# Building the one-hots of four groups in seven: slot by slot on GpSimd and turned in two-byte words, instead of compared with broadcast places on VectorE

## What is computed

```python
h = jnp.maximum(_layernorm(x, axis=-1), 0.0)
x = x + jax.ops.segment_sum(h[src], dst, num_segments=6250)
h = jnp.maximum(_layernorm(x, axis=-1), 0.0)
y = out = h
for l in range(3):
    f1 = jax.nn.relu(y[row] @ nb_W[l] + nb_b[l])
    f2 = jax.nn.relu(y[col] @ self_W[l] + self_b[l])
    a = jax.nn.relu(jnp.concatenate([f1, f2], axis=1) @ att1_W[l] + att1_b[l])
    mask = jnp.clip(jax.nn.sigmoid((a @ att2_W[l] + att2_b[l])[:, 0]) * 1.5 - 0.45, 0.0, 1.0)
    rowsum = jax.ops.segment_sum(mask, row, num_segments=n) + 1e-06
    d = jnp.clip(rowsum ** (-0.5), 0.0, 10.0)
    y = jax.ops.segment_sum((mask * d[row] * d[col])[:, None] * y[col], row, num_segments=n)
    out = out + y
x = x + out            # row = src, col = dst
```

## Time and profile before

| | us |
|---|---|
| median of 3 runs (lowest, highest) | 4028.7 (4028.5, 4032.4) |
| the profiled execution | 4025.1 |
| its span in the profile | 4023.2 |
| sort, about | 60 to 480 |
| build and first hop, about | 500 to 1105 |
| three layers, about | 1140 to 4009 |

### The profile page before, as it was taken

How to read it: one execution, slowest core, us unless ns; L and a number is a source line. 1 busy time by engine, 2 the same in 40 slices (tenths; PEclk the granted TensorE clock), 3 DMA queues, 4 the chain that set the end, 5 groups by cost and what they waited for, 6 DMA issues and landing times. The chain is left out here.

```text
span 4023.2 us, 257999 instructions
## 1 busy us (share of the span) xinstructions
PE 3711.7 (92%) x99855; PEld 3565.5 (89%) x99856; DVE 3262.2 (81%) x5362; ACT 1976.7 (49%) x5432; POOL 2380.6 (59%) x4693
## 2 busy tenths in 40 slices
PE   5999678888879999999998999999998999999998
PEld 4888578888859999899988999999997999989998
DVE  7999868888768888788877888878886888878887
ACT  1222368888721111488871111178884111138887
POOL 2777523333235666677774666667775566667776
PEclk8989799999989999999999999999999999999999
DMA  1111189999837777677745777757773677767775
GB/s 38 16 16 16 26 282 335 342 339 338 308 100 249 248 240 244 196 190 190 191 133 193 244 248 248 249 158 190 190 191 120 234 247 240 245 198 190 191 190 153
DMA packets 586269, 800.05 MB, mean 199 GB/s; under 512 B 126790, under 2 KB 528154, under 8 KB 586170
## 3 DMA queue, kind: packets, MB, share of 16 engines
q1 hardware_dynamic: 550106, 719.89, 57.3%
q0 software_dynamic: 36064, 78.85, 6.6%
HBM read 672.34 MB, written 126.04 MB: 198 GB/s over the span
## 5 line engine op out<-in xcount | busy, mean ns | idle before, releaser
L1372 PE MATMUL pre_ps<-rows_a,hot_ab 128*128 128x64 bf16 x21609 | 1298.3, 193 | 46.7 <-ACT rows_a L1465 23.2
L1372 PE MATMUL pre_ps<-table,hot_ab 128*128 128x64 bf16 x21609 | 1296.9, 193 | 1.1 <-issue 1.1
L1372 PEld LDWEIGHTS pre_ps<-rows_a,hot_ab 128*128 128x128 fp8e4 x21609 | 1128.2, 98 | 75.9 <-issue 52.8
L1606 POOL TENSOR_TENSOR message<-message 128x448 f32<-128x448 f32 x1029 | 947.2, 932 | 318.3 <-DVE message L1674 317.7
L1372 PEld LDWEIGHTS pre_ps<-table,hot_ab 128*128 128x128 fp8e4 x21609 | 1130.8, 98 | 0.6 <-issue 0.6
L1656 DVE SCALAR_TENSOR_TENSOR message<-pre_ps,all_w 128x448 f32<-128x448 f32 x1029 | 642.8, 625 | 276.9 <-PE pre_ps L1372 200.3
L1416 PE MATMUL pre_ps<-table,hot_ab 128*128 128x64 bf16 x21609 | 803.0, 193 | 19.6 <-DVE message L1674 9.0
L1416 PEld LDWEIGHTS pre_ps<-table,hot_ab 128*128 128x128 fp8e4 x21609 | 761.7, 98 | 22.1 <-issue 21.6
L1513 ACT ACTIVATE message<-pre_ps 128x448 bf16<-128x448 f32 x1029 | 673.6, 675 | 164.9 <-DVE pre_ps L1668 136.7
L1668 DVE TENSOR_TENSOR pre_ps<-pre_ps,mask 128x448 f32<-128x448 f32 x735 | 464.9, 633 | 205.1 <-PE pre_ps L1416 182.9
L1639 DVE TENSOR_REDUCE logit<-message 128x7 f32<-128x448 f32 x1029 | 626.4, 609 | 0.0
(11 more groups left out here) (195 smaller groups left out, 4844.7 us busy)
## 6 DMA issues: line engine op xcount, KB each, us to landing
hot_ab<-hot_scratch SPq DMA_DIRECT2D x2058, 224.0 KB, 4.0
hot_scratch<-hot SPq DMA_DIRECT2D x343, 336.0 KB, 5.9
both<-hot_scratch SPq DMA_DIRECT2D x147, 784.0 KB, 5.1
places<-slots_scratch POOLq DMA_DIRECT2D x196, 224.0 KB, 6.4
places<-slots_scratch POOLq DMA_DIRECT2D x98, 336.0 KB, 7.2
slots_scratch<-bins SPq DMA_DIRECT2D x392, 16.0 KB, 1.4
out<-res SPq DMA_DIRECT2D x1, 1536.0 KB
raw<-in_src SPq DMA_DIRECT2D x1, 768.0 KB
```

The source lines that it names most:

```text
L1372: last = nc.tensor.matmul(pre_ps[g][:, j, :], hot[:, b, g, end, j * P:(j + 1) * P].bitcast(FP8), table, start=end + part == 0, stop=end == ...
L1606: pool.tensor_tensor(message[:, g, :, 2, :], message[:, g, :, 1, :], top[:, g, :, 1, :, 1], ALU.subtract).then_inc(s["third_ready"], 1)
```

## The change

In the groups `COMPARED` = 1, 3, 5 and 6 the row end takes another way.

- *Sort.* ScalarE copies the row half of `bins_ps` a second time, to `row_bins` (bf16); TensorE turns it with an identity (`turn_slots`); ScalarE puts the result into `slot_place`, which keeps for all rows and columns the place of each slot, with the slot on the partition.
- *Build, GpSimd.* `fetch_places` takes one row of `slot_place` (49 values). For each compared unit seven `tensor_scalar` compare `iota1` (1 to 128) with the place of the partition's slot, is-equal and then times 56. That gives part 2, slot by node, directly (`row_slots`). `load` takes the row end of the first group of each chunk alone, and stands behind the compares.
- *TensorE.* In a compared unit `turn` turns part 2 with `pack_two` (128 x 64) into numbers of two bytes, 7 matmuls. `turn_other`, a step later, turns the other end as before, 7 matmuls.
- *VectorE.* `find` compares only the other end (896 bytes). `take_pairs`, a step later, converts the 448 two-byte words to part 0 (`row_nodes`).
- *ScalarE* converts 224 words of such a unit (part 3), and all its jobs, the counts, the sums and the adds come one step later than before.
- SyncE's store waits for `row_slots` and `row_nodes` too.

```diff
                     act.wait_ge(stored[b], nth * (16 * COPIES))
+                    nc.scalar.activation(row_bins[:, b, :], bins_ps[b][0:HALF, :], ACT.Copy)
                     nc.scalar.activation(bins[:, b, :], bins_ps[b][:, :], ACT.Copy).then_inc(s["bins_ready"], 1)
...
+                def turn_slots(c, b):
+                    pe.wait_ge(s["bins_ready"], c + 3)
+                    pe.wait_ge(s["slots_taken"], c + 2)
+                    hold_waits(pe, s)
+                    nc.tensor.matmul(slots_ps[b][:, :], row_bins[:, b, :], k.identb[0:HALF, 0:HALF],
+                                     start=True, stop=True).then_inc(s["slots_turned"], 1)
...
+    COMPARED = (1, 3, 5, 6)
...
                 def load(c, h, r):
                     a, z = chunks[c]
-                    for e in range(2):
-                        tile = k.slots_dram[:, bass.ds(r + e * k.HALF, 1), a * G:z * G, :]
+                    for e, last in ((0, a + 1), (1, z)):
+                        tile = k.slots_dram[:, bass.ds(r + e * k.HALF, 1), a * G:last * G, :]
...
+                def find_slots(n):
+                    if n.g == COMPARED[0]:
+                        fetch_places(n)
+                        pool.wait_ge(s["places_ready"], n.r + 1)
+                    reused(pool, n)
+                    at_least(pool, s["counted"], n.u - NG + 1)
+                    hold_waits(pool, s)
+                    for j in range(G):
+                        last = pool.tensor_scalar(hot[:, n.slot, ROW_SLOT, j * P:(j + 1) * P], k.iota1[:, :], place_of(n, j),
+                                                  float(HOT), ALU.is_equal, ALU.mult)
+                    last.then_inc(s["row_slots"], 1)
...
+                def step(recent):
+                    if recent[0] is not None and recent[0].g in COMPARED:
+                        find_slots(recent[0])
+                    if recent[2] is not None:
+                        next_load(recent[2])
+                each_unit(pool, k, 3, step)
...
                 def turn(n):
                     pe.wait_ge(s["hotT"], n.u + 1)
                     at_least(pe, s["hot_ready"], n.u - 1)
+                    if n.g in COMPARED:
+                        pe.wait_ge(s["row_slots"], compared(n))
...
+                    if n.g in COMPARED:
                         for j in range(G):
+                            last = nc.tensor.matmul(pair_ps[n.half][:, j, :], hot[:, n.slot, ROW_SLOT, j * P:(j + 1) * P].bitcast(FP8),
+                                                    k.pack_two[:, :], start=True, stop=True)
...
+                def turn_other(n):
+                    if n.g in COMPARED:
+                        pe.wait_ge(s["row_nodes"], compared(n))
...
-                    for n, do in zip(recent, (turn, count, add_up)):
+                    for n, do in zip(recent, (turn, turn_other, count, add_up)):
...
-                    for n, do in zip(recent, (take_words, take_counts)):
+                    for n, do in ((recent[1], take_words), (recent[2], take_counts)):
...
+                def take_pairs(n):
+                    if n.g in COMPARED:
+                        dve.wait_ge(s["turned"], n.u + 1)
+                        reused(dve, n)
+                        dve.tensor_copy(hot[:, n.slot, ROW_NODE, :].bitcast(U16), pair_ps[n.half].rearrange("p j w -> p (j w)"))\
+                            .then_inc(s["row_nodes"], 1)
...
-                    for n, do in ((recent[0], find), (recent[3], add_in)):
+                    for n, do in ((recent[0], find), (recent[1], take_pairs), (recent[4], add_in)):
```

More of the change, by code:

```diff
@@ L10 @@
 U8 = mybir.dt.uint8
+U16 = mybir.dt.uint16
 ALU = mybir.AluOpType
@@ L373, in sort_edges @@
         bins_ps = [ps(f"bins_ps{i}", [2 * HALF, P]) for i in range(2)]
+        slots_ps = [ps(f"slots_ps{i}", [P, HALF]) for i in range(2)]
         by_column = hot[:, :, :, :, :].rearrange("p b a g n -> p b (a g) n")
@@ L553, in _ @@
                     dve.sem_inc(s[name], 2)
+                nc.vector.memset(row_bins[:, :, :], 0.0)
                 def pick_blocks(c, b):
@@ L879, in build_and_sum, with compared @@
     WORDS = P // 4
+    ROW_NODE, OTHER_NODE, ROW_SLOT, OTHER_SLOT = range(4)
+    COMPARED = (1, 3, 5, 6)
+    LOADS = [(NB + 1) // 2, (NB + 1) // 2 + 1]
+    def compared(n):
+        before = sum(g < n.g for g in COMPARED)
+        if n.alone:
+            return before + (n.g in COMPARED)
+        return n.i * (2 * len(COMPARED)) + (len(COMPARED) + 2 * before + (n.h + 1) * (n.g in COMPARED))
     chunks = [(a, min(a + 2, NG)) for a in range(0, NG - 1, 2)]
@@ L917, in _ @@
                     load(c, 0, 1)
[L918 to L925, removed]
+                def step(recent):
[4 more added lines that the diff above has]
+                each_unit(pool, k, 3, step)
+                for c in range(len(chunks)):
+                    for h in range(2):
+                        pool.wait_ge(places_in[c][h], LOADS[h] * 32)
             @block.sync
@@ L950, in turn @@
                     at_least(pe, s["hot_ready"], n.u - 1)
+                    if n.g in COMPARED:
+                        pe.wait_ge(s["row_slots"], compared(n))
                     hold_waits(pe, s)
-                    for end in range(2):
+                    if n.g in COMPARED:
                         for j in range(G):
-                            last = nc.tensor.matmul(word_ps[n.half][:, end, j, :],
-                                                    hot[:, n.slot, end, j * P:(j + 1) * P].bitcast(FP8), k.pack[:, :],
-                                                    start=True, stop=True)
-                    last.then_inc(s["turned"], 1)
+                            last = nc.tensor.matmul(pair_ps[n.half][:, j, :], hot[:, n.slot, ROW_SLOT, j * P:(j + 1) * P].bitcast(FP8),
+                                                    k.pack_two[:, :], start=True, stop=True)
+                    else:
+                        for end, of in enumerate((ROW_NODE, OTHER_NODE)):
+                            for j in range(G):
+                                last = nc.tensor.matmul(word_ps[n.half][:, end, j, :], hot[:, n.slot, of, j * P:(j + 1) * P].bitcast(FP8),
+                                                        k.pack[:, :], start=True, stop=True)
+                    last.then_inc(s["turned"], 1)
+                def turn_other(n):
+                    if n.g in COMPARED:
+                        pe.wait_ge(s["row_nodes"], compared(n))
+                        hold_waits(pe, s)
+                        for j in range(G):
+                            last = nc.tensor.matmul(word_ps[n.half][:, 1, j, :], hot[:, n.slot, OTHER_NODE, j * P:(j + 1) * P].bitcast(FP8),
+                                                    k.pack[:, :], start=True, stop=True)
+                        last.then_inc(s["other_turned"], 1)
                 def count(n):
@@ L1788, in gnn @@
         allocate(nc, k, st)
[L1789 to L1795, removed]
+        with ExitStack() as slots_st:
+            allocate_slots(nc, k, slots_st)
+            with ExitStack() as sort_st:
+                allocate_sort(nc, k, sort_st)
+                constants(nc, k)
+                load_inputs(nc, k, src, dst, x)
+                sort_edges(nc, k)
+            first_table(nc, k)
+            build_and_sum(nc, k)
         spilled_edges(nc, k, [(nodes(k, k.cur), k.rows_a_dram)], [(k.rows_a_dram, k.srci)], k.dsti, nodes(k, k.res), k.D, "hop")
```

84 lines of the change are left out of this document (66 added, 18 removed).

## The result

The changed kernel takes 4753.7 us (median of 4, 4749.7 to 4762.6) against 4028.6: 1.180 times the time before, 95% interval 1.1785 to 1.1817. The profiled execution has a span of 4748.0 us, 724.8 more than before. Between the first find and the last add into `res` the build took 605.9 us before (499.6 to 1105.5) and takes 1346.1 now (470.9 to 1817.0), + 740.2. The sort in front ends 28.7 us earlier; everything behind the build takes 13.3 us more, 6 of them before the first layer; the others were not traced to a cause. 740.2 - 28.7 + 13.3 = 724.8.

The account below looks back on a forecast made before the run. The prediction took a VectorE-TensorE loop of 11.8 us a row as the bound before and GpSimd after: 16.6 + 4.5 blocking = 21.1 us, + 456 us over 49 rows, giving 4485 us, range 4010 to 4800.

Parts of the forecast that it names:

- What bounds before: Build stage before the change: a closed loop of VectorE and TensorE, not the DMA, sets 11.8 us a row.
- Sort at 0, its exposed bound + 25 us: Sort: one added matmul and two ScalarE copies a row hide in ScalarE's idle time; all exposed, 25 us.
- VectorE: Build: a compared group's find falls from 1.1 to 0.65 us, the added cast takes 0.62; VectorE gains nothing.
- GpSimd's compare: Build: 28 compares of 128 elements a row on GpSimd, 0.433 us each, ends 0.24 and 0.625.
- compares near 0.65: Sign in the build that the prediction is wrong, against its right sign of 0.43 to 0.48 us each.
- two operations cost two: Rival: GpSimd's compare goes at the max-min rate, 0.625 us; 22.0 us a row, 26.5 blocked; 4529 to 4749 us; chance 0.25.
- Blocking, 4.5 us a row: Build: VectorE's finds hold up GpSimd, each for its length less 0.19 us; bounds 0 and 5.9 us a row.
- GpSimd's issues and fetch, 4.5: Build, rest of GpSimd's row: six issues 3.5 us, a fetch 0.4, some seven waits 0.6; together 4.5 us.
- Clock: Build: even at half speed TensorE's unit costs 2.9 us, just under 3.0, so nothing is added.
- The sum: Build: 16.6 + 4.5 = 21.1 us a row against 11.8, + 456 us over 49 rows; forecast 4485 us.
- The rival that GpSimd fits: Rival: at copy rate, unblocked, GpSimd needs 11.2 us a row, so the old loop binds; 4022 us; chance 0.25.
- Bound by GpSimd, but cheaply: Rival: GpSimd bounds the build at multiply-add or copy rate, or without blocking; 4073 to 4294 us; chance 0.20.

Follow-up runs that it names:

- no_groups: The changed kernel with no compared group, no compare on GpSimd and all places broadcast: 4012.3 us, 0.995 of the kernel before.
- no_finds: The changed kernel with VectorE's finds comparing 8 bytes of each end instead of 896: 4572.2 us against 4753.7, run once.
- one_group: The changed kernel with only group 3 compared, 7 compares a row, and all places broadcast: 4249.8 us, 1.054 times the kernel before.

## Why the prediction was right in direction and short in size

- **What bounds before.** Nothing speaks against it, but no run tests it alone. That the DMA share of 0.97 did not set the pace rests on the waits; `no_groups` keeps 23.9 us for two rows with the same transfers, and where the share fell to 0.38 GpSimd was the bound.
- **Sort at 0, its exposed bound + 25 us.** The sign was wrong: - 28.7 us, by TensorE's clock. The prediction had the 0.88 of the sort in a row and never asked what an extra matmul does to it.
- **VectorE.** Find 0.765 instead of 0.65 and cast 0.624 as taken; no effect, since neither bounds.
- **GpSimd's compare.** Here the size was lost. I took the comparison's row, 0.433 us a compare; undisturbed it is 0.691 from start to start, and "compares near 0.65" was the prediction's own sign of being wrong. The term of 12.1 us a row is 19.3, which in 49 rows is 354 us more. The forecast fell short by 269; the sort's gain and smaller terms below took 85 back. The rival *two operations cost two*, with max-min's 0.625, is the one that came true; it had a chance of 0.25, the forecast 0.30. That its blocked end, 4749 us, is 5 us from the median is in part luck: it has 26.5 us a row, where 27.3 were measured, and leaves out the sort's gain and the saved start. Its reason is half of the cause: of the 227 ns between 478 and 705, 114 are the second operation (591 against 705), and 113 the comparison itself. Of the overlap, 0.045 taken, 0.014 was there.
- **Blocking, 4.5 us a row.** Right in kind and close in size: 28 x 0.094 + 6 x 0.21 = 3.9 by the means, 3.7 by `no_finds`. By the Trainium skill's rule ("SBUF — State Buffer", Who interferes with whom) it would be the whole length of the finds, 3 x 1.19 + 4 x 0.765 = 6.6; the trace has less. That a find can pass beside the part of GpSimd's work that needs no port would explain it; no run shows that.
- **GpSimd's issues and fetch, 4.5.** The remainder is 27.3 - 19.3 - 3.9 = 4.1; priced by rows it is 6 x 0.59 + 0.24 + 0.38 = 4.2.
- **Clock.** Taken at no cost. It fell to 0.66 and TensorE's busy time rose from 517 to 699 us in the build, but GpSimd was full and waited 1.5 us for TensorE in all, so it stayed off the path.
- **The sum.** 19.3 + 3.9 + 4.1 = 27.3 a row, + 15.5 x 49 = + 760 from the row periods, against + 740 between first find and last add: the build's start cost 26 us beyond the loop before and 6 now. The forecast had 21.1 a row, adds 6.0 us apart and a build of about 1060 us; measured are 27.3, 7.8 and 1346.
- **The rival that GpSimd fits** is out: it needed 0.26 us a compare, and 0.691 is 2.7 times that. The body at 1.03 cycles an element of the Trainium skill ("GPSIMD Engine Reference", 3.1) does not fit: the runs show 3.3 ns an element for is-equal and multiply, against the 0.77 of the copy that agreed with it. *Bound by GpSimd, but cheaply* is out for the same reason. The threshold that I gave for this rival, GpSimd's row under 11.8 us, was wrong by itself: `one_group` was under it and lost 5 us a row.

## What to carry to other kernels

Price a step that moves to another engine from a row with the same kind and number of operations, and where none exists give the dearest near form its full weight: here the middle was taken, and the dearest, max-min, was the nearest. Sum the receiving engine's queue, and then ask how early it can begin: an in-order pipeline exposes the whole latency of a step that starts with the unit that needs it, even on an engine with time to spare. A stage whose granted clock goes up and down is worth a one-line test with an added matmul, at more than one place.

## What was not expected of the hardware

- GpSimd's `tensor_scalar`, 128 two-byte elements with a scalar from SBUF and byte output: 705 ns for is-equal and multiply, 591 for is-equal, 362 for multiply-add. Instructions without a wait between them overlap by 14 ns only (705 against 691 from start to start).
- One 64-column matmul of 0.2 us per row in front of the scatter kept TensorE at 2.4 GHz for some 350 us and made the kernel 0.8% faster; behind the scatter it did nothing.
